# Stacked queries and keys by way of an image in DRAM instead of twelve direct copies

## The reference, cut to what matters

```
def _self_attention(q, k, v, mask):
    scale = 1.0 / math.sqrt(q.shape[-1])
    scores = jnp.einsum('bthd,bshd->bhts', q, k * scale) + mask
    attn = jax.nn.softmax(scores, axis=-1)
    return jnp.einsum('bhts,bshd->bthd', attn, v)
context = _self_attention(q, k, v, mask)
for _ in range(REPETITIONS - 1):
    context = _self_attention(context, k, v, mask)
```

## Time and profile before

| | |
|---|---|
| three runs | 4277.9, 4292.6 and 4299.11 us, median 4292.6 us |
| the profiled execution | 4289.5 us, its span 4287.7 us |
| PE busy | 3253.4 us (76%) |
| DVE busy | 2780.6 us (65%) |
| ACT busy | 2072.2 us (48%) |
| granted PE clock, mean | 0.859 |
| direct copies to the stacks | 1212 of 64 KB and 576 of 32 KB from SP, 12 of 64 KB from ACT |

### The profile page before, as it was taken

The page is one execution under the profiler, slowest core; times in us unless marked ns, Lnnn a source line. Parts: engine busy times, 40 slices in busy tenths (PEclk is TensorE's granted clock), DMA queues, the critical chain, the costliest instruction groups (busy, mean ns, idle before and its releaser), DMA issues. The chain is left out here.

```text
span 4287.7 us, 91912 instructions
## 1 busy us (share of the span) xinstructions
PE 3253.4 (76%) x33230; PEld 2220.6 (52%) x33230; DVE 2780.6 (65%) x7659; ACT 2072.2 (48%) x4656; POOL 1180.7 (28%) x2276
## 2 busy tenths in 40 slices
PE   6886888895888676948888888766983479859992
PEld 2443555463555346834554555433553456658992
DVE  5884776274787485647776777566785458955563
ACT  2664666223443444525666666543661134325661
POOL 2322221011111134640101010134321431233565
PEclk9987999797998688968999999777995599979996
DMA  4423331033220431331212020142322140122332
GB/s 89 68 34 59 58 57 27 15 95 48 32 37 11 58 70 59 88 61 29 45 23 45 21 43 25 29 65 46 58 46 67 52 127 20 37 72 79 108 97 65
DMA packets 321188, 232.56 MB, mean 54 GB/s; under 512 B 45975, under 2 KB 305668, under 8 KB 320560
## 3 DMA queue, kind: packets, MB, share of 16 engines
q1 hardware_dynamic: 306948, 199.40, 23.2%
q0 software_dynamic: 12928, 26.50, 2.1%
q10 hardware_dynamic: 864, 0.79, 0.1%
HBM read 69.21 MB, written 55.63 MB: 29 GB/s over the span
## 5 line engine op out<-in xcount | busy, mean ns | idle before, releaser
L1411 ACT ACTIVATE PT<-ps 128x512 f32<-128x512 f32 (+1 forms) x1600 | 811.5, 559 | 423.7 <-PE ps L1347 331.2
L1361 DVE TENSOR_REDUCE M<-ps 128x2 f32<-128x512 f32 x1024 | 652.8, 683 | 227.6 <-PE ps L1347 200.4
L1313 PE MATMUL ps<-SKB 51*128 51x256 bf16 (+3 forms) x3584 | 419.6, 280 | 184.5 <-DMA SKB<-HH 76.9
L1358 DVE TENSOR_REDUCE M<-ps 128x3 f32<-128x384 f32 x768 | 389.7, 549 | 128.5 <-PE ps L1347 66.2
L1504 PE MATMUL ps<-PT,VA 128*9 128x256 f32 (+1 forms) x7168 | 466.6, 381 | 1.4 <-ACT PT L1411 1.2
L1451 PE MATMUL ps<-SKB 53*128 53x256 bf16 (+3 forms) x3584 | 365.9, 273 | 72.8 <-DMA SKB<-MT 46.8
L3881 ACT ACTIVATE SKB<-ps,SKB 128x128 f32<-128x128 f32 x1032 | 295.3, 370 | 250.5 <-PE ps L3799 249.8
L1347 PE MATMUL ps<-tri,idh 64*128 64x128 bf16 x5120 | 400.4, 227 | 0.0
L1313 PEld LDWEIGHTS ps<-SKB 51*128 51x128 bf16 (+1 forms) x3584 | 131.0, 96 | 459.5 <-DVE M L1361 154.6
L3945 DVE COPY SKB<-SKB 128x1028 f32 (+1 forms) x258 | 186.9, 725 | 228.5 <-PE ps L3808 197.3
L1347 PEld LDWEIGHTS ps<-tri,idh 64*128 64x128 bf16 x5120 | 282.4, 101 | 33.3
(11 more groups left out here) (501 smaller groups left out, 6236.3 us busy)
## 6 DMA issues: line engine op xcount, KB each, us to landing
SKB<-HH SPq DMA_DIRECT2D x1212, 64.0 KB
SKB<-HH SPq DMA_DIRECT2D x576, 32.0 KB
PT<-L_sorted_rows SPq DMA_DIRECT2D x258, 64.0 KB
L_sorted_results<-SKB SPq DMA_DIRECT2D x258, 64.0 KB
SKB<-in_L3f_w SPq DMA_DIRECT2D x32, 256.0 KB, 3.7
L_sorted_rows<-TV SPq DMA_DIRECT2D x2, 4032.0 KB, 29.0
SKB<-scratch SPq DMA_DIRECT2D x2, 2048.0 KB, 11.0
SKB<-in_L1f_w SPq DMA_DIRECT2D x16, 256.0 KB, 3.2
```

What stands on the lines that cost most here:

```text
L1313: k = e.matmul(self.mx_bank(m + i)[:, o:o + n], K.QS[self.set(c)][64 * i:64 * i + rows, s, 256 * bb + 128 * qt:256 * bb + 128 * qt + 128], ...
L1358: k = e.tensor_reduce(K.M3[n % 2][:, hh, 0:3], mx[:, 0:384].rearrange("p (a k) -> p a k", a=3), axis=AX.X, op=ALU.max)
L1361: k = e.tensor_reduce(K.M3[n % 2][:, hh, 0:2], mx.rearrange("p (a k) -> p a k", a=2), axis=AX.X, op=ALU.max)
L1411: e.activation(K.PT[:, x % 4, n * i:n * i + n], self.st_bank(x, i)[:, 0:n], ACT.Exp, bias=0.0, scale=self.scale).then_inc(*self.exp.inc())
```

## The change

The blocks go to their stacks by way of DRAM. `sp_image` writes each part, as often as it is needed, to its places in an image of 6 x 128 x 512 (or 256) bf16 in DRAM: one transfer for the high part with three places, one for the mid part with two, one for the low part. `sp_stack` waits for the three, and reads the image back in two transfers of 48 partitions each, one for either half of the heads. A block so takes 5 transfers, all from SP. There are three images, used in turn like `HH`. The read stands two slots behind the image (one slot in s4 and s7). The waits that protect the stack (`qk_free`, `freed`) now stand ahead of the read alone. In s6 the split of "rep" begins one slot earlier (`OOS` instead of `OOS + 1`). `SPLIT_K` is reordered, so that the places of one part have one distance. `act_share` is gone.

```diff
-SPLIT_K = (0, 1, 2, 0, 1, 0)
+SPLIT_K = (1, 0, 2, 0, 1, 0)
...
+        self.images = [nc.dram_tensor(f"stack_image{i}", (6 * 128 * 512,), BF16).ap() for i in range(3)]
...
-        self.stacked = K.landings("stacked", 3, n, 12)
+        self.stacked = K.landings("stacked", 3, n, 5)
...
+    def image(self, n, w):
+        return self.K.images[n % 3][0:768 * w].rearrange("(s p k) -> s p k", s=6, p=128)
+
+    def imaged(self, n):
+        sem, landed = self.stacked.at(n)
+        return sem, landed - 2 * 16
+
+    def sp_image(self, e, n, order, w=512):
         h = self.K.HH[n % 3]
+        rows = self.image(n, w).rearrange("s p k -> p s k")
+        for part, ready in enumerate((self.hi, self.mid, self.lo)):
+            at = [s for s in range(6) if order[s] == part]
+            by = at[1] - at[0] if len(at) > 1 else 1
+            e.wait_ge(*ready.at(n))
+            e.dma_start(rows[:, at[0]:at[-1] + 1:by, :], h[:, part:part + 1, 0:w].to_broadcast([128, len(at), w])
+                        ).then_inc(*self.stacked.inc(n))
+
+    def sp_stack(self, e, n, dst, pitch=48):
         w = dst.shape[2]
-        if steps[0] == 0:
-            e.wait_ge(*self.mid.at(n))
-            e.wait_ge(*self.lo.at(n))
-        for s in steps:
-            for par in halves:
-                r = pitch * par + 8 * s
-                e.dma_start(dst[r:r + 8, :, :], h[64 * par:64 * par + 64, order[s], 0:w]).then_inc(*self.stacked.inc(n))
+        e.wait_ge(*self.imaged(n))
+        for par in range(2):
+            e.dma_start(dst[pitch * par:pitch * par + 48, :, :],
+                        self.image(n, w)[:, 64 * par:64 * par + 64, :].rearrange("s (d b) k -> s d b k", b=8)
+                        ).then_inc(*self.stacked.inc(n))
...
-                rows.append((s + self.OOS + 1, "rep", u))
+                rows.append((s + self.OOS, "rep", u))
...
-        for step in range(3):
-            u = self.at(g, 2 + step)
-            if u is not None and self.cross:
-                self.sp_split(e, self.split_of["xq", u], "xq", u, step)
-            u = self.at(g, self.OOS + 2 + step)
-            if u is not None and self.units[u][1] < self.reps - 1:
-                self.sp_split(e, self.split_of["rep", u], "rep", u, step)
-        for step in range(self.stack_slots):
-            c = self.first_at.get(g - self.QSTK - step)
+        for off, kind, lag in ((2, "xq", 2), (self.OOS + 1, "rep", 2)):
+            u = self.at(g, off)
+            if u is not None and (kind, u) in self.split_of:
+                self.sp_split_image(e, self.split_of[kind, u], kind)
+            u = self.at(g, off + lag)
+            if u is not None and (kind, u) in self.split_of:
+                self.sp_split_stack(e, self.split_of[kind, u], kind, u)
+        for off, kind in ((self.QSTK, "q"), (self.KSTK, "k")):
+            c = self.first_at.get(g - off)
             if c is not None:
-                self.sp_split(e, self.split_of["q", c], "q", c, step)
-            c = self.first_at.get(g - self.KSTK - step)
+                self.sp_split_image(e, self.split_of[kind, c], kind)
+            c = self.first_at.get(g - off - 2)
             if c is not None:
-                self.sp_split(e, self.split_of["k", c], "k", c, step)
+                self.sp_split_stack(e, self.split_of[kind, c], kind, c)
```

More of the change, by code:

```diff
@@ L959, in sp @@
                 if s == 0:
+                    self.st.sp_image(e, n, SPLIT_K)
+                if s == 2:
                     self.st.prev.freed(e, n)
-                if 0 <= s < 6:
-                    self.st.stack(e, n, SPLIT_K, K.QS[n], steps=[s])
+                    self.st.sp_stack(e, n, K.QS[n])
             yield
@@ L993, in __init__ @@
         self.QSTK, self.KSTK = (-26, -17) if cross else (-20, -12) if reps > 1 else (-14, -20) if gate else (-20, -14)
-        self.stack_slots = 3 if reps > 1 else 6
         self.plan(units, start, L, start[-1] + self.OUT + 12)
@@ L1047, in __init__ @@
         self.rows_to = None
-        self.shared = 2 if mode == "bias" else 0
         self.logits = None
@@ L1054, in __init__ @@
         self.rows_at = {36 + 8 * c: c for c in range(8)}
-        self.share_at = self.splits[1][0] + 2
     def plan_splits(self):
@@ L1184, in qk_free, with sp_split_image, sp_split_stack @@
             e.wait_ge(*self.bias.anti.at(15 if self.set(c) == 2 else 7))
[L1186 to L1190, removed]
+    def sp_split_image(self, e, n, kind):
+        self.sp_image(e, n, SPLIT_K if kind == "k" else SPLIT_Q, 512 if kind in ("q", "k") else 256)
+    def sp_split_stack(self, e, n, kind, key):
         K = self.K
[L1192 to L1195, removed]
+        if kind in ("q", "k"):
+            self.qk_free(e, key)
+            if key < 3:
                 self.sp_stack_rows(e, kind, key)
[L1197 to L1203, removed]
+            self.sp_stack(e, n, (K.QS if kind == "q" else K.KS)[self.set(key)], 64)
         elif kind == "xq":
             bb = key % 2
-            if step == 0 and key >= 2:
+            if key >= 2:
                 e.wait_ge(*self.scored(self.nx * (key - 2) + 9))
-            self.stack(e, n, SPLIT_Q, K.QX[:, :, 256 * bb:256 * bb + 256], 48, [2 * step, 2 * step + 1])
+            self.sp_stack(e, n, K.QX[:, :, 256 * bb:256 * bb + 256])
         else:
             c, bb = self.units[key][0] // 2, self.units[key][0] % 2
[L1211 to L1220, removed]
+            e.wait_ge(*self.scored(self.nx * key + 7))
+            self.sp_stack(e, n, K.QS[self.set(c)][:, :, 256 * bb:256 * bb + 256], 64)
     def sp_stack_rows(self, e, kind, c):
@@ L1743, in act_slot @@
             self.logits.act_logits(e, self.logits_at[g])
-        if self.shared and g == self.share_at:
-            for n, (_, kind, key) in enumerate(self.splits[:self.shared]):
-                self.act_share(e, n, kind, key)
     def dve_slot(self, e, g):
@@ L2104, in act_q, with sp_q_image, sp_q_stack @@
         k.then_inc(*self.ff.inc())
[L2106 to L2115, removed]
+    def sp_q_image(self, e, c):
+        self.sp_image(e, c + 2, SPLIT_Q)
+    def sp_q_stack(self, e, c):
+        if c >= 4:
+            e.wait_ge(*self.scored(c - 4))
+        elif c == 1:
+            self.prev.done(e)
+        elif c > 1:
+            e.wait_ge(*self.setup.k1.at(c - 2))
+            e.wait_ge(*self.setup.k2.at(c - 2))
+        self.sp_stack(e, c + 2, self.Q[c % 4])
     def pe_scores(self, e, b, k):
@@ L2326, in sp_slot @@
             self.sp_shift(e, b, self.Q[b // 2 % 4], b % 2)
-        for step in range(3):
-            c = self.stack_at.get(g - step)
-            if c is not None:
-                self.sp_q(e, c, step)
+        c = self.stack_at.get(g)
+        if c is not None:
+            self.sp_q_image(e, c)
+        c = self.stack_at.get(g - 1)
+        if c is not None:
+            self.sp_q_stack(e, c)
         if g == self.P + 8:
```

1 line of the change is left out of this document (removed).

## The result

| | before | after |
|---|---|---|
| median of the runs | 4292.85 us (4) | 4195.49 us (4) |
| ratio | | 0.977, 95% interval 0.975 to 0.980 |
| span of the profiled execution | 4287.7 us | 4191.5 us |
| mean granted clock of PE | 0.859 | 0.865 |

What follows compares the result with a forecast made beforehand. Waits between engines bound the kernel, PE's for stacks and maxima making 184 us. Terms summed to 144 us, less 19 us for waits meeting others, 125 us: 4289.5 to 4164.5, stated as 4165 us, range 4090 to 4265.

Steps and rivals of the forecast that it cites:

- SP: SP's issuing of a block falls from 8.3 to 2.7 us, with 0.45 us plus a 0.08 us gap per transfer.
- The read of a wide block: The two reads of a 512 wide block run on six engines at 112 GB/s, 7.0 us for the pair.
- s6: Repetition blocks in s6: the wait for the stack goes and the clock rises, 2.3 us in each of 29 units, 67 us.
- s0 and the start of s3: First stacks: two wide blocks take 18.9 against 26.0 us, saving 7.1 us in s0 and 2.5 at s3's start.
- s1: Of 38.7 us of waits in s1, 25 us go because SP's backlog goes.
- s3's maxima and ACT: In s3 ACT gets its buffer earlier and 8.87 us of issuing back, so PE's wait for maxima falls by 9 us.
- s4 and s7: Half of the remaining waits for stacks (22.2 us) and maxima (21.4 us) go, 22 us.
- Deduction for ends of waits that meet others: Outside s6, a quarter of the 77 us, 19 us, is taken off because shortened waits meet others just behind them.
- Rivals 1 and 2: Rival 1: another chain sets s6's pace, 4237 us, chance 0.16; rival 2: two DRAM passes no faster, 4285 us, 0.09.
- Rival 3: Reads run on six engines at 8.2 GB/s each, making the kernel slower, 4427 us; chance 0.09.

Runs made afterwards that it cites:

- e1: Changed kernel with the image laid out so that writes and reads use all 16 DMA engines, eight transfers a block; 4109.91 us, ratio 0.958 to the kernel before.
- e5: Changed kernel with the split, image and reads of s6's repetitions one slot later; 4308.85 us, ratio 1.005 to the kernel before.
- e9: Kernel before, twelve direct copies kept, with the split and copies of s6's repetitions one slot earlier; ratio 0.995.
- e12: Kernel before with direct copies' partitions 6 apart, repetitions' split and copies one slot earlier, each copy waiting only for its own part; 4078.8 us, ratio 0.950.
- e6: Kernel before with each direct copy's 8 partitions 6 apart, not adjacent; 4168.46 us, ratio 0.972.

## Why the prediction was right, and where not

The sign, the mechanism of the largest term and the range were right; the sum was 125 us for a measured 96 to 97. By its steps:

- **SP: right.** 2.9 us a block, said 2.7. The issue of a read (0.765 us) was dearer than the 0.45 taken, the writes as assumed.
- **The read of a wide block: right.** 104 GB/s at share 0.36, said 112 on six engines. So the rule on the number of engines (the Trainium skill, "DMA: Bandwidth & Descriptors", section "Why a DMA increments its semaphore by 16 and not by 1") holds here. It was cited as speaking against the change, and e1 shows how much it cost: 2% of the kernel.
- **s6: mechanism right, size too small.** Said 67 us, measured 86 in the stretch. The plain unit is 13.08 us where I said about 14; the 0.65 us kept for new small waits was not needed there, and the clock is full there. Units with wide blocks beside them take longer. PE's waits for the stack in s6 are 1.1 us (52.2 before). The waits for maxima in s6 rose from 9.2 to 24.1 us, which I had not foreseen. I had also put the gain down to the low part being ready 2 us earlier. e5, e9 and e12 show that it is SP's order: what leaves ahead of the maxima, and whether SP is free when they come.
- **s0 and the start of s3: this is the step that failed.** "Two blocks back to back: 18.9 against 26.0 us". Measured 25.5 in s0, counted as the working does from the first low part to PE's start, where the kernel before has 26.1. The working gave the image 2.7 us to land, and only the reads queued behind each other. The second image stands behind the first read on the engines that both use: from the end of its issue to the second read it takes 9.4 us. The second read itself, from issue to PE's use, takes 10.7 us in s0 and 10.4 in s3, where 0.5 + 7.0 + 1.7 = 9.2 were said. In s3 the first scores came at 1002.3 (1001.2 before) for the same reason: the second read was issued at 991.88. 10.5 us forecast for the two starts; none in s3, 1.1 in s0.
- **s1: the wrong reason.** "SP's backlog goes", 25 us. SP's backlog did go. PE's waits for cross stacks fell with it from 16.9 to 10.0 us, but its waits for the maxima there are 22.1 us, as before (21.8). So SP was not their cause. In e6, where SP issues as many copies as before and only the transfers are faster, they fall to 3.0 us. I had the row for it (share 0.57 at 66 GB/s) and used it only for the pace of blocks, not for what a small transfer meets behind one.
- **s3's maxima and ACT: nothing came.** I took 9 us there, since ACT would get its buffer back earlier. ACT begins the block at 1031.13 in both kernels, still behind the landing of a stack, and PE uses the maxima at 1036.63 before and 1036.73 after.
- **s4 and s7:** 22 us said. The stretch of s4 and s5 is 6.8 us shorter, that of s7 and s8 2.3 us longer.
- **Deduction for ends of waits that meet others:** a quarter of 77 us. Outside s6 the change gave 10 us of the 77. It was not ends meeting: the waits themselves hardly went. PE's waits for stacks and maxima together went from 13.0 to 21.7 us in s0, from 38.7 to 32.1 in s1, from 25.7 to 28.6 in s3, from 22.6 to 14.4 in s4, and from 23.0 to 20.7 in s7 and s8: 123.0 before, 117.5 after. So the 125 us came as near to the 96 as they did by luck in part: s6 gave 19 us more than its term, and the other stages 48 less than theirs.
- **Rivals 1 and 2.** No other chain sets the pace of s6 before 13.08 us; e12, with all of this off the path, has the same plain unit. The kernel before has one too (OT at 1970.81 and at 1983.89), ahead of its first wait for a stack in s6. Rival 2 (two passes through DRAM are no faster than twelve copies) was wrong for the kernel and near the truth for the transfer: e5 has 10.6 against 9.6 us for a narrow block, s0 25.5 against 26.1 for two wide ones.
- **Rival 3 (slower; the reads at 8.2 GB/s an engine)** was wrong, and its counter-argument, that the old copies crowd into 8 partitions, was the most valuable sentence of the prediction. e6 shows that spreading the partitions alone is worth 2.8% of the kernel before. The text used it to defend the new reads and didn't ask what it meant for the old copies.
- Of what the profile was to show: the stack's wait under 5 us in s6 (1.1), a clock near 0.98 (0.97 over 600 us) and a share of 0.38 (0.36) came, and units of about 14 us in plain stretches; maxima under 8 us in s1 did not (22.1), nor rows of 0.45 us for the reads (0.77).

## What to carry to other kernels

When a transfer shows a high share of the DMA engines at a low rate, first change where its pieces land, before changing how many transfers there are: one stride gave 2.8% here. Here a large transfer held back the small ones issued behind it, from SP and from ACT alike, so count what the loop needs next into the same sum. On an engine that works in order, give each issue only the wait that it needs, and look at what stands between it and the latency-critical small one.

## What the hardware did that I had not expected

- With copies of 64 KB into 8 adjacent partitions a busy DMA engine moved 7.2 GB/s, with 8 partitions 6 apart 17.4 GB/s, from the same source in the same pieces of 1 KB.
- The issue of a transfer on SP took 0.61 us for 8x8x512, 0.45 us (median) for writes of 128 partitions, and for the reads 0.77 us with six pieces in the outer step, 0.42 us in e1, whose source steps evenly over the 48 partitions. That the shape is the reason was not tested.
- A 786 KB read moved 105 GB/s on six engines and 193 GB/s on sixteen, so 18 and 13 GB/s a busy engine.
- Two copies of maxima, 16 KB in all, were used 8.4 us after their issue behind a 786 KB read on six engines, and issuing the maxima from ACT did not shorten PE's waits for them (96.3 us in all, 85.6 from SP).
